# Running sums of the graph-attention layers as one scan per chunk of edges

## The reference, cut to what matters

```
e      = leaky_relu(a_own[dst] + a_other[src])          # one score per edge and head
w      = exp(e - max over the node's edges of e)
out[n] = sum over the node's edges of w * x[src]  /  sum of w
```

## Time and profile before

| | |
|---|---|
| median of 3 runs | 10274.1 us (10271.78 to 10276.29) |
| profiled execution | 10270.59 us, its span 10268.9 us |
| DVE busy | 6511.5 us (63%) in 19179 instructions |
| POOL busy | 6508.4 us (63%) in 6186 |
| PE, ACT busy | 3047.2 us (30%), 2898.0 us (28%) |
| "heads" stage, first gather to last scatter | 5823.4 to about 7235.5 us |
| "edge" stage, first gather to last scatter | 7263.1 to about 8265.5 us |

### The profile page before, as it was taken

How to read it: one execution, slowest core, us unless ns; L and a number is a source line. 1 busy time by engine, 2 the same in 40 slices (tenths; PEclk the granted TensorE clock), 3 DMA queues, 4 the chain that set the end, 5 groups by cost and what they waited for, 6 DMA issues and landing times. The chain is left out here.

```text
span 10268.9 us, 93901 instructions
## 1 busy us (share of the span) xinstructions
PE 3047.2 (30%) x15231; PEld 2833.1 (28%) x15231; DVE 6511.5 (63%) x19179; ACT 2898.0 (28%) x8170; POOL 6508.4 (63%) x6186
## 2 busy tenths in 40 slices
PE   3233002111116666203666444444100012222300
PEld 2132001111115666203555344444100012222200
DVE  8999877666656676203666599999323258777700
ACT  5365234333333444101333222222100012222200
POOL 2333027777767777576777667777677765555377
PEclk6665555555557887655555555555555555555555
DMA  1010361111114544213555311111111123333211
GB/s 52 16 29 28 119 203 25 25 25 25 25 26 130 160 153 151 95 43 109 174 173 176 107 45 47 49 47 42 43 45 45 42 77 95 91 93 94 77 46 39
DMA packets 455134, 791.83 MB, mean 77 GB/s; under 512 B 119921, under 2 KB 149610, under 8 KB 454558
## 3 DMA queue, kind: packets, MB, share of 16 engines
q1 hardware_dynamic: 252126, 560.13, 16.4%
q0 software_dynamic: 188448, 201.53, 9.2%
q10 hardware_dynamic: 14112, 26.10, 0.7%
HBM read 388.06 MB, written 425.04 MB: 79 GB/s over the span
## 5 line engine op out<-in xcount | busy, mean ns | idle before, releaser
L1060 POOL DMA_INDIRECT e_other<-X,e_from_rows x392 | 611.4, 1560 | 283.5 <-DVE e_fin L1361 147.2
L1738 POOL DMA_INDIRECT e_mine<-T,e_from_rows x392 | 400.8, 1022 | 570.1 <-DVE e_from_rows L1785 451.5
L743 POOL COPY sort_spare<-sort_words 128x768 f32<-128x768 f32 x272 | 369.4, 1381 | 606.9 <-DVE sort_words L802 395.7
L3407 POOL DMA_INDIRECT e4s_mine<-XA,e4s_from_rows x392 | 385.2, 983 | 477.7 <-ACT e4s_kept L3817 355.1
L2227 PE MATMUL e_turned<-ident,e_own_x 128*128 128x128 f32 x196 | 54.5, 434 | 1573.5 <-ACT e_own_x L2139 1573.5
L3428 POOL DMA_INDIRECT out_rows<-e4s_out,e4s_to_rows x392 | 386.0, 985 | 210.3 <-issue 210.3
L2375 POOL DMA_INDIRECT e_mine<-X,e_from_rows x392 | 403.8, 1030 | 174.7 <-issue 112.9
L2396 POOL DMA_INDIRECT G<-e_g_slot,e_to_rows x392 | 386.0, 985 | 181.0 <-issue 119.1
L2882 POOL DMA_INDIRECT X<-e_row,e_to_rows x392 | 422.8, 1079 | 119.4 <-issue 118.5
L3873 PE MATMUL e4s_n_result<-w_pair,e4s_n_p_t 128*128 128x128 f32 x784 | 202.0, 439 | 991.4 <-DVE e4s_n_y L3703 600.7
L1075 POOL DMA_INDIRECT X<-e_row,e_to_rows x392 | 403.4, 1029 | 141.0 <-issue 118.2
(11 more groups left out here) (708 smaller groups left out, 15940.6 us busy)
## 6 DMA issues: line engine op xcount, KB each, us to landing
XA<-e_n_xa SPq DMA_DIRECT2D x49, 1056.0 KB, 5.3
e4s_n_xa<-XA SPq DMA_DIRECT2D x49, 1056.0 KB, 6.5
X<-e_n_row SPq DMA_DIRECT2D x49, 576.0 KB
T<-pl_row SPq DMA_DIRECT2D x98, 272.0 KB
X<-e_n_row SPq DMA_DIRECT2D x49, 528.0 KB, 3.1
X<-pl_x ACTq DMA_DIRECT2D x98, 260.0 KB, 2.7
e_n_x<-X SPq DMA_DIRECT2D x49, 520.0 KB, 5.7
G<-e_n_g SPq DMA_DIRECT2D x49, 512.0 KB, 2.9
```

Source lines behind the costliest of these rows:

```text
L1060: gp.indirect_dma_start(out=other[:, h, j, :], out_offset=None, in_=others[:, :], in_offset=bass.IndirectOffsetOnAxis(ap=from_rows[:, h, 1 ...
L1738: gp.indirect_dma_start(out=mine[:, h, j, :], out_offset=None, in_=g.T0[:, :], in_offset=bass.IndirectOffsetOnAxis(ap=from_rows[:, h, 0, j ...
```

## The change

In `attend_edges`, for both kinds, features and columns are exchanged in the tiles of the running sums, and the 8 x (heads + 1) instructions of a chunk become one scan. A scan (TENSOR_TENSOR_SCAN with multiply and add) computes `out[i] = factors[i] * out[i-1] + pay[i]` along the free dimension. Each feature gets 9 places: place 0 has factor 0 and the value carried from the chunk before, places 1 to 8 are the columns. So `pay`, `factors` and `sums` are [128, 256, 9] ("edge": [128, 64, 9]), and one scan runs over 2304 (576) elements.

- `pay` is written feature by feature (step of 9 floats between neighbours of the inner loop); `scaled` and ACT's copy read `sums` with the same step (`sums_of`).
- ACT writes `factors`: after `ex` one more activation (Copy) that repeats the factors of a head for its 64 features, 2048 (512) elements, before `squares_of`.
- DVE copies the carried column (256 or 64 elements, step 9 on both sides) into `pay`.
- `head` is kept by a masked copy over a whole chunk: `heads` is [128, 256, 8], and the mask `ends` is `g.head_end`, nonzero at most in the one column of a partition that ends its first node. It is done one chunk late (`heads_of(last, ...)`), before the scan. Weights and maxima go to a tile `tail` of their own with a masked copy of 64 (16) elements.
- After the last chunk a reduction over the columns of `heads` and `head_tails` yields `head`.
- The two copies of flags per chunk (`same`, `first`) are gone; one copy of 8 flags (`ends`) is new. More tiles are cleared at the start (`factors` with 4608 or 1152 elements, `heads`, `sums`).

```diff
@@ lay_out_edges
+                    v.tensor_copy(g.head_end[s][:, T - 1:], g.first[s][:, T - 1:])
+                    v.tensor_tensor(g.head_end[s][:, 0:T - 1], g.first[s][:, 0:T - 1], g.first[s][:, 1:], ALU.subtract)
@@ attend_edges, tiles
-        pay = sb("pay", [P, J, WACC])
-        state = sb("state", [P, RING, J, WSTATE])
-        head = sb("head", [P, WSTATE])
+        pay, factors = sb("pay", [P, WACC, J + 1]), sb("factors", [P, 2, WACC, J + 1])
+        sums, tail = sb("sums", [P, RING, WACC, J + 1]), sb("tail", [P, RING, J, 2 * H])
+        heads, head_tails = sb("heads", [P, WACC, J]), sb("head_tails", [P, J, 2 * H])
...
+        def sums_of(h, count):
+            return sums[:, h, :, 1:count + 1].rearrange("p k j -> p j k")
@@ row_numbers
-                    v.tensor_copy(same[:, h, :], g.same[s][:, bass.ds(n * J, J)])
-                    v.tensor_copy(first[:, h, :], g.first[s][:, bass.ds(n * J, J)]).then_inc(...)
@@ pay_out
+                        acc.done(v.tensor_tensor(pay[:, :, 1:].rearrange("p (q d) j -> p j q d", d=D),
+                                                 ot[:, :, WOTHER - D:].unsqueeze(2).to_broadcast([P, J, H, D]),
                                                  ex[:, b, 1, :, :].unsqueeze(3).to_broadcast([P, J, H, D]), ALU.mult), "pay")
@@ running_sums
+                    heads_of(last, 1 - b)
                     need("pay")
-                    for j in range(J):
-                        before = state[:, h, j - 1, :] if j else state[:, last, J - 1, :]
-                        if j:
-                            need(f"head{(j - 2) % J}")
-                        for q in range(H):
-                            part = slice(q * D, (q + 1) * D)
-                            run = v.scalar_tensor_tensor(out=state[:, h, j, part], in0=before[:, part], scalar=ex[:, b, 0, j, q:q + 1],
-                                                         in1=pay[:, j, part], op0=ALU.mult, op1=ALU.add)
-                        acc.done(run, f"run{j}")
-                        acc.done(v.copy_predicated(head[:, :], first[:, h if j else last, j - 1:j or J].to_broadcast([P, WSTATE]), before), f"head{(j - 1) % J}")
+                    acc.done(v.tensor_copy(pay[:, :, 0:1], sums[:, last, :, J:]), "carry")
+                    acc.done(v.tensor_copy(ends[:, b, :], g.head_end[s][:, bass.ds(n * J, J)]), "ends")
+                    need("carry")
+                    v.wait_ge(act.sem, act.after(n, "factors"))
+                    acc.done(v.tensor_tensor_scan(sums[:, h, :, :].rearrange("p k j -> p (k j)"), factors[:, b, :, :].rearrange("p k j -> p (k j)"),
+                                                  pay[:, :, :].rearrange("p k j -> p (k j)"), 0.0, ALU.mult, ALU.add), "run")
+
+                def heads_of(h, b):
+                    v.copy_predicated(head_tails[:, :, :], ends[:, b, :].unsqueeze(2).to_broadcast([P, J, 2 * H]), tail[:, h, :, :])
+                    acc.done(v.copy_predicated(heads[:, :, :], ends[:, b, :].unsqueeze(1).to_broadcast([P, WACC, J]), sums[:, h, :, 1:]), "head")
@@ scaled
-                    end_dve.done(v.tensor_tensor(by_head(z[:, 0, 0:count, :]), by_head(state[:, h, 0:count, 0:WACC]),
+                    end_dve.done(v.tensor_tensor(by_head(z[:, 0, 0:count, :]), by_head(sums_of(h, count)),
@@ ACT, attend
                     act.done(a.activation(ex[:, b, :, :, :], lows[:, b, :, :, :], ACT.Exp), "ex")
+                    need(act, "ex")
+                    if begun(c, 2):
+                        a.wait_ge(acc.sem, acc.after(n - 2, "run"))
+                    act.done(a.activation(factors[:, b, :, 1:].rearrange("p (q d) j -> p q d j", d=D),
+                                          ex[:, b, 0, :, :].rearrange("p j q -> p q j").unsqueeze(2).to_broadcast([P, H, D, J]), ACT.Copy), "factors")
@@ ACT, "edge"
-                        out_copied.done(a.activation(sent[:, h, :, D + 2:], state[:, h, :, :], ACT.Copy))
+                        a.activation(sent[:, h, :, D + 2:2 * D + 2], sums_of(h, J), ACT.Copy)
+                        out_copied.done(a.activation(sent[:, h, :, 2 * D + 2:], tail[:, h, :, :], ACT.Copy))
```

More of the change, by code:

```diff
@@ L938, in attend_edges @@
         to_rows = sb("to_rows", [P, RING, J], I32)
-        first = sb("first", [P, RING, J], I32)
-        same = sb("same", [P, RING, J])
+        ends = sb("ends", [P, 2, J], I32)
         mine = None if kind == "edge" else sb("mine", [P, RING, J, WOWN])
@@ L984, in attend_edges @@
             "heads": "sadd score keep top fall fallen rise"}[kind]), \
-            Engine(sem(f"{name}_act"), "square root ln1 ln2 ex" if kind == "hyper" else "ex")
-        acc = Engine(sem(f"{name}_acc"), "pay weight " + ("count " if kind == "hyper" else "") + "tops " + RUN_STEPS)
+            Engine(sem(f"{name}_act"), "ex factors")
+        acc = Engine(sem(f"{name}_acc"), "pay weight tops head carry ends run")
         if kind == "heads":
@@ L1070, in body @@
                         else:
-                            gp.wait_ge(acc.sem, acc.after(n, f"run{J - 1}"))
+                            gp.wait_ge(acc.sem, acc.after(n, "run"))
                         gp.wait_ge(to_ready[h], k + 1)
@@ L1097, in _ @@
                 v.memset(top[:, RING - 1, :, :], NEG)
-                v.memset(head[:, :], 0.0)
-                v.memset(first[:, :, :], 0)
+                v.memset(heads[:, :, :], 0.0)
+                v.memset(head_tails[:, :, :], 0.0)
+                v.memset(ends[:, :, :], 0)
+                v.memset(factors[:, :, :, :], 0.0)
+                v.memset(tail[:, RING - 1, :, :], 0.0)
                 if kind == "hyper":
                     v.memset(ones[:, :], 1.0)
-                v.memset(state[:, RING - 1, :, :], 0.0).then_inc(set_up, 1)
+                v.memset(sums[:, RING - 1, :, :], 0.0).then_inc(set_up, 1)
                 v.wait_ge(set_up, 1)
@@ L1405, in need @@
                     v.wait_ge(engine.sem, engine.after(0, step))
[L1407 to L1409 removed]
+                v.wait_ge(acc.sem, acc.after(NCH - 1, "run"))
+                v.tensor_copy(end_state[:, 0:WACC].unsqueeze(2), sums[:, LAST, :, J:])
+                v.copy_predicated(head_tails[:, :, :], ends[:, LAST % 2, :].unsqueeze(2).to_broadcast([P, J, 2 * H]), tail[:, LAST, :, :])
+                v.copy_predicated(heads[:, :, :], ends[:, LAST % 2, :].unsqueeze(1).to_broadcast([P, WACC, J]), sums[:, LAST, :, 1:]).then_inc(heads_held, 1)
+                v.wait_ge(heads_held, 1)
+                v.tensor_copy(end_state[:, WACC:], tail[:, LAST, J - 1, :])
+                v.tensor_reduce(head[:, 0:WACC], heads[:, :, :], AX.X, ALU.add)
+                v.tensor_reduce(head[:, WACC:], head_tails[:, :, :].rearrange("p j k -> p k j"), AX.X, ALU.add).then_inc(set_up, 1)
                 v.wait_ge(set_up, 2)
@@ L3962, in gnn_kernel @@
         g.index = [sb(f"index{s}", [P, 3, T + 1], I32) for s in range(ORDERS)]
-        g.first = [sb(f"first{s}", [P, T], I32) for s in range(ORDERS)]
+        g.first, g.head_end = ([sb(f"{q}{s}", [P, T], I32) for s in range(ORDERS)] for q in ("first", "head_end"))
         g.pen, g.contrib, g.same = ([sb(f"{q}{s}", [P, T]) for s in range(ORDERS)] for q in ("pen", "contrib", "same"))
```

35 lines of the change are left out of this document (14 added, 21 removed).

## The result

The changed kernel takes 10499.83 us (median of 4 runs, 10498.56 to 10502.75), the kernel before 10272.94 (4 runs, 10270.99 to 10276.29). The ratio is 1.0222, 95% interval 1.0205 to 1.0238. The profiled execution took 10498.56 us, its span is 10496.9 us. The forecast was 10473.

A forecast was written before the change was run, and what follows sets the result against it. It took DVE to bound "heads" (27.45 us a chunk, POOL 25.5) and POOL "edge"; 159 + 25 + 15 = +199 us on 10270.6 gave 10470, timed 10473 us. Its own range was 10380 to 10580, 8 in 10 within 10240 to 10700.

The forecast's parts named there:

- POOL takes over as the bound: In "heads": POOL's round grows from 25.5 to 30.7 us, above DVE's 26.7; +159 us for the stage.
- two signs of being wrong: In "heads": DMAs inside the scan taking 1 us, or POOL still waiting for DVE at its first gather in most rounds.
- The wait before `scores`: In "heads": DVE would stand idle before `scores`, waiting for gathered rows; no size given.
- The hold of L - 1.0 us: A DVE instruction of length L with two SBUF inputs costs POOL L - 1.0 us: scan 3.8, masked copy 1.4.
- Strides at no cost: `pay` written and `sums` read with 36 bytes between neighbours: taken as zero, upper end 2.2 us per instruction.
- The first rival: Strided steps are slow: `pay` and L1395 take 4.5 us instead of 2.3; total 10704 us; chance 0.14.
- ScalarE's factors: ACT, before `squares` in "heads": 1.9 us, costing DVE's round 1.4 us, which vanish in POOL's shadow.
- The doubling that I named as possible: ACT's factors in "heads": broadcast input and short rows could double the cost.
- Scan and masked copy: DVE in "heads", per chunk: scan over 2304 elements 4.8 us, masked copy of 2048 elements 2.43 us.
- the small masked copy: DVE in "heads", per chunk: adds 0.15 us after overlap.
- "edge": POOL stays the bound; the scan, and now and then the masked copy, hold it 0.5 us a chunk: +25 us.
- once: Clearing more elements at the start (7.6 us) and closing copies, reductions and flags (7): +15 us, ends 5 and 20.

The follow-up runs named there:

- e1: Changed kernel with ScalarE's squares moved ahead of ex and factors: ratio 1.0154 to the kernel before, 32.37 us a chunk in "heads".
- e5: Changed kernel, squares ahead of factors, scan cut into one piece per head: ratio 1.0122 to the kernel before, 29.49 us a chunk in "heads".
- e4: Kernel before, with a block (the probe) ahead timing operations at steps of 1 to 9 floats and gathers beside long VectorE instructions; kernel before: 11513 us there.
- e2: Changed kernel with 4 of the 8 scatters of a chunk left out in "heads": ratio 1.011 to the kernel before, 31.27 us a chunk.
- e11: Changed kernel, factors read from a turned copy of ex, "edge" factors in PSUM: ratio 1.0209 to the kernel before, 32.78 us a chunk in "heads".
- e7: e5 with `pay`, `z0` and masked copy also cut by head, factors read from turned ex: 10291.8 us, ratio 1.0019 to the kernel before.
- e8: Kernel before with ScalarE's factors alone added, written to a tile nothing reads: ratio 1.0165, 30.90 us a chunk in "heads".
- e6: Changed kernel, squares first, "heads" scan in five pieces with constant PSUM factors: ratio 1.0138 to the kernel before, 29.47 us a chunk.
- e12: The changed kernel again, unedited, on a slower chip: ratio 1.0176 to the kernel before, 32.32 us a chunk in "heads".
- e9: Kernel before with only the once-a-chunk masked copy (four pieces in "heads"), flag copies gone, waits changed: ratio 0.9948, 26.46 us a chunk.

## Why the prediction was right, and where it was not

**POOL takes over as the bound: right, but by 0.65 us and not by 4.** e1 (VectorE's idle time moves, the round stays) and the rows of POOL show it. Neither of the two signs of being wrong came: transfers inside the scan took 4.7 us, and POOL waited for VectorE's `e_fin` in 4 rounds. The wait before `scores` was forecast as the rule and came in 22 rounds. A transfer of 4.71 us in the scan and one of 2.58 in the masked copy are the ones forecast (4 to 5.5, 2 to 3).

**The hold of L - 1.0 us: right for long instructions.** The scan (4957 ns) charged 3.8 us, the masked copy 1.6 (forecast 1.4). It is wrong as a sum over pieces: four scans of 1.34 us charge together about 0.3 us instead of 1.4 (e5).

**Strides at no cost: wrong, 3.0 us a round on VectorE and as much on POOL.** I judged 2048 elements by 16 in rows 9: at the 0.72 ns more per element that e4 shows, 16 elements cost 12 ns, too little to be told from 175 against 171. In "heads" this is the +80 us: 30.7 forecast, plus 1.5 for each of two instructions, gives 33.7 for POOL. (VectorE's round grows by the same 3.0.) Its rows give 1622 / 49 = 33.1, and the time from `pay` to `pay` is 32.30, since the scatters of the last chunks come after the last `pay`. The first rival had the mechanism and half as much again in size: 2.2 us an instruction for 1.5, and a total of 10704.

**ScalarE's factors: 3.76 us instead of 1.9, and the cover nearly gone.** The prediction let it vanish under POOL. It did, but the VectorE chain with it is 31.65 us and not 26.7, so the cover was about 1 us thick (e2) and not 4. The doubling that I named as possible came from reading `ex` across heads, as e11 (1911 ns) shows.

**Scan and masked copy: right.** 4.96 us (forecast 4.8), 2.47 (2.43), the small masked copy 0.22 (0.15), the carry 0.39 (0.35). The Trainium skill (DVE: opcode table, instruction layouts, handler registers and perf-mode slots, "Datapath and trigger behaviour", on feedback) says that the built-in scan runs at half throughput. The probe agrees: 2.29 us for 1024, TENSOR_TENSOR 1.23.

**"edge" +30 (forecast +25), once about +3 (forecast 15).** In "edge" the scatters went from 995 to 1045 ns and the gathers from 956 to 984: 0.62 us a chunk, the forecast's 0.5. In "heads" the clears run from 5815.4 to 5825.0 us, 9.6 instead of 2.6 (5819.8 to 5822.4), so they cost what was forecast; but they begin 4.3 us sooner, and only 3 us of them reach the first gather. Why they begin sooner was not looked into.

**The last layer: -43 us, not foreseen; that the total came within 27 us is luck.** Without it the change would have cost some 270 us, where 199 were forecast. The largest wait for "issue" on VectorE in that layer makes up 39 of the 43 (us in total, times, longest), first of the kernel before, then of the changed one:
```profile
DVE e4s_n_small L3714 <- issue: 43.2, 9, 5.9
```
```profile
DVE e4s_small L3639 <- issue: 4.5, 2, 2.3
```
The experiments on the chip that ran at the same speed line up with it. Largest "issue" wait of VectorE in the last layer against its length: 4.5 us and 2013 (changed), 8.6 and 2011 (e7), 24.7 and 2037 (e5), 43.2 and 2056 (before), 45.3 and 2057 (e8), 69.5 and 2066 (e6). The layer's own code is the same in all. Only what stands ahead of it differs, so I think that its place in the program decides, but no run moved it alone. Nor is it the kernel alone: on the slower chips the same changed kernel took 2061 us there (e12, with 53.2 us of such waits before one line where it had 4.5), and the kernel before 2058 (e4).

## What to carry to other kernels

Count a long VectorE instruction twice when both inputs are in SBUF and GpSimd issues transfers beside it: once on VectorE, and its length less 1 us on GpSimd. Cut such instructions into pieces about as long as one transfer takes (here 1.3 us; e7's pieces, with a shorter ScalarE chain, took 4.4 us off a round), or put one operand in PSUM (seen in the probe; in e6 it gained no more than pieces did). Before a layout is turned for one instruction, price the step of its neighbours: in the probe, from 4 floats on, a TENSOR_TENSOR on VectorE paid 1.6 times and an activation on ScalarE 1.9 times, while a scan paid nothing. And when two engines' rounds are within 1 us of each other, an edit to one alone shows nothing.

## What the runs showed of the hardware that was not expected

- A scan takes the same 2.29 us for 1024 elements at steps of 1 to 9 floats, where TENSOR_TENSOR goes from 1.23 to 1.97. A COPY of 1024 at steps of 9 on both sides takes 1.08.
- With one operand in PSUM POOL was not held at all: gathers of 0.94 us inside a scan of 4.42. The Trainium skill (SBUF — State Buffer, "Who interferes with whom") has one port pair, shared by the two engines, as the only thing they contend for. The trace fits that, and goes against the inference there that `tensor_tensor` doesn't stall the generation of descriptors: 3.56 and 3.75 us where 0.94 is undisturbed.
- Unchanged code in the last layer took 2011 to 2066 us in six kernels that differ only ahead of it, 0.5% of the kernel: as much as the best version here gains (e9, 0.5%). Its last layer took 2090 us on its chip, where e12 took 2061, so that gain isn't due to it.
